# First feed-forward product of the second phase from rounded parts and residues: three float32r products in place of one float32 product

## The reference, cut to what matters

```python
def _layer(x, wqkv, qs, ksc, wo, lg, lb, w1, b1, w2, b2):   # x: (8, 1024, 256), run twice
    ...
    x = x + o @ wo                                   # local attention, output projection
    h = shift_token(x)
    mu = h.mean(-1, keepdims=True)
    var = h.var(-1, keepdims=True)
    h = (h - mu) / jnp.sqrt(var + 1e-05) * lg + lb   # layer norm, 256 channels
    h = h @ w1 + b1                                  # 256 -> 2 * 682, the product that is changed
    a, g = jnp.split(h, 2, axis=-1)
    h = a * jax.nn.gelu(g, approximate=False)
    x = x + h @ w2 + b2
    return x
```

## Time and profile before

| what | value |
|---|---|
| median of 3 runs | 5651.63 us (5647.0 to 5652.35) |
| profiled execution, span | 5649.7 us |
| PE busy | 5488.2 us, 97% of the span |
| DVE, ACT, POOL busy | 73%, 61%, 17% |
| second phase | from about 2711 us to the end |
| second phase, 2840 to 5560 us | PE busy 2699.66 of 2720 us, granted clock 1.00 |

### The profile page before, as it was taken

One profiled execution on the slowest core, in us unless ns is written; L12 is line 12 of the kernel. 1 busy time (PEld: TensorE's weight loads), 2 busy tenths in 40 slices (PEclk: granted clock), 3 DMA queues, 4 the chain that ended last, 5 costly groups with the idle time before them and its releaser, 6 DMA issues.

```text
span 5649.7 us, 145780 instructions
## 1 busy us (share of the span) xinstructions
PE 5488.2 (97%) x57776; PEld 2674.3 (47%) x57776; DVE 4147.2 (73%) x10780; ACT 3455.2 (61%) x6979; POOL 934.9 (17%) x1905
## 2 busy tenths in 40 slices
PE   8999999999999999999799999999999999999998
PEld 3444444444444444433355555555555555555553
DVE  5888878787887888788566666666666777777774
ACT  4676666676666766666455655556555565555654
POOL 2222222222222222222000000000000001010100
PEclk9999999999999999999899999999999999999998
DMA  3333333233333333333100000000000000000000
GB/s 70 55 55 69 54 59 60 50 74 55 65 55 59 63 51 71 55 58 78 44 12 16 8 16 12 12 16 8 16 32 17 18 19 16 19 16 19 19 16 19
DMA packets 128519, 215.62 MB, mean 38 GB/s; under 512 B 40032, under 2 KB 40160, under 8 KB 127072
## 3 DMA queue, kind: packets, MB, share of 16 engines
q1 hardware_dynamic: 127840, 206.30, 18.0%
HBM read 45.73 MB, written 25.17 MB: 13 GB/s over the span
## 4 chain that ended last, share of the span: by engine, by line
PE 72%; ACT 11%; issue 10%; DVE 3%; POOL 3%; DMA 0%; POOLq 0%; SPq 0%; ACTq 0%; DVEq 0%
PE ps L571 23%; PE ps L700 14%; PE ps L821 10%; PE ps L1042 6%; PE ps L1005 5%; PE ps L906 3%; ACT pt L1259 3%; PE ps L898 3%; PE ps L923 3%; ACT gates L1457 1%; ACT sm L1376 1%; PE ps L1007 1%; PE ps L873 1%; PE ps L882 1%; POOL both L2101 1%
## 5 line engine op out<-in xcount | busy, mean ns | idle before, releaser
L1259 ACT ACTIVATE pt<-ps 128x1024 f32<-128x1024 f32 (+7 forms) x2048 | 1237.2, 653 | 620.9 <-PE ps L571 462.9
L700 PE MATMUL ps<-pt,va 128*32 128x512 f32 (+3 forms) x3072 | 1227.5, 487 | 19.9 <-POOL pt L2076 19.9
L700 PE MATMUL ps<-pt,ones 128*32 128x512 f32 (+3 forms) x6144 | 1237.0, 489 | 0.0
L700 PE MATMUL ps<-pt,vs 128*32 128x512 f32 (+3 forms) x3072 | 1231.0, 489 | 0.0
L1633 DVE CUSTOM_DVE_ANT_0 junk<-ps,causal 128x128 bf16<-128x128 f32 (+3 forms) x2048 | 977.8, 487 | 307.2 <-PE ps L571 291.2
L571 PE MATMUL ps<-kt,qt 96*32 96x512 bf16 (+3 forms) x12288 | 1017.0, 329 | 34.9 <-DVE mc L1633 15.9
L571 PE MATMUL ps<-qt,kt 98*32 98x512 bf16 (+3 forms) x12288 | 835.7, 328 | 22.0 <-ACT pt L1259 21.0
L1637 DVE TENSOR_REDUCE mc<-ps 128x1 f32<-128x512 f32 x1024 | 706.3, 690 | 159.2 <-PE ps L571 128.5
L2076 POOL TENSOR_SCALAR_AFFINE_SELECT pt<-pt 128x256 f32<-128x256 f32 x1024 | 467.2, 456 | 1941.1 <-ACT pt L1259 1939.5
L821 PE MATMUL ps<-wqkv,xs 128*128 128x512 f32 x1536 | 727.9, 603 | 0.0
L1376 ACT ACTIVATE sm<-sm,mxw 128x256 f32<-128x256 f32 (+1 forms) x1024 | 493.5, 484 | 241.0 <-DVE mxw L1802 239.6
(11 more groups left out here) (149 smaller groups left out, 8537.9 us busy)
## 6 DMA issues: line engine op xcount, KB each, us to landing
qt<-part SPq DMA_DIRECT2D x768, 64.0 KB, 2.4
kt<-part SPq DMA_DIRECT2D x768, 64.0 KB, 2.5
ya<-wy SPq DMA_DIRECT2D x128, 128.0 KB, 2.3
yb<-wy SPq DMA_DIRECT2D x128, 128.0 KB, 2.3
xs<-between_phases SPq DMA_DIRECT2D x32, 512.0 KB, 3.8
xt<-in_x SPq DMA_DIRECT2D x16, 512.0 KB, 6.5
between_phases<-z SPq DMA_DIRECT2D x16, 512.0 KB, 2.8
between_phases<-xo SPq DMA_DIRECT2D x16, 512.0 KB, 2.8
```

Source lines behind the costliest of these rows:

```text
L700: mmi = pe.matmul(ps[32 * q:32 * q + 32, 4 + half, lo - half * 512:hi - half * 512], w, probs(kb)[:, i, lo - first(kb):hi - first(kb)], st ...
L1259: act.activation(probs(kb)[:, i, kb * P - first(kb):1024 - first(kb)], ps[:, 2 * i:2 * i + 2, :].rearrange("p a q -> p (a q)")[:, kb * P:1 ...
```

## The change

The layer-normed activations and the weights `w1` are both split in two: a part rounded to the type float32r (`cnh`, `w1h`) and the residue to the float32 value, also float32r (`cnl`, `w1l`). One float32 product becomes three products in float32r: part by part, residue of the weights by part, and part by residue of the activations. One tile of two `kc` thus takes six products, 66 for a half. The six are cut in two pieces of three (`W1_PRODUCTS`), which stand where the two `kc` stood, so all other steps of PE keep their places.

New work: ACT runs `scale_bias` four times in place of two (rounded, then float32 in place, for each `kc`); POOL subtracts for each half (`residue`, two of 128x512, in place over `cn`), ahead of the gate window's `combine`, and for each layer splits the weights (`split_w1`, two copies and two subtractions of 128x1408). New waits: the first gate tile waits for both rounded parts (`cnh_done`, signalled after the first and the third of ACT's four steps) and for the weights' residue (`w1l_done`); its second piece waits for both residues (`cnl_done`). The new tiles lie over old ones (`w1l` over `w1`, `cnl` over `cn`, `cnh` over `sqf`); so ACT's step also waits for `ssum_done`.

```diff
+W1_PRODUCTS = (((0, 0, 0, 0), (0, 1, 0, 1), (1, 0, 0, 2)), ((1, 1, 0, 3), (0, 0, 1, 4), (0, 1, 1, 5)))
...
+        w1h = sb("w1h", [P, 2, 2 * HB - 1, P], F32R)
+        w1l = over("w1l", "w1", [P, 2, 2 * HB - 1, P], F32R)
+        cnh = over("cnh", "sqf", [P, 2, 512], F32R)
+        cnl = over("cnl", "cn", [P, 2, 512], F32R)
...
+            def normed(m, n, to, tile, width, parts):
+
+                for part_of in parts:
+                    if n == 0 and part_of == 1:
+                        pe.wait_ge(cnl_done, done(2 * m + 2))
+                    for w, kc, x, k in W1_PRODUCTS[part_of]:
+                        mmi = pe.matmul(to, (w1h, w1l)[w][:, kc, tile, 0:width], (cnh, cnl)[x][:, kc, :],
+                                        start=k == 0, stop=k == 5)
+                return mmi
...
                 elif j == 0:
-                    pe.wait_ge(w1_ready, sent(m // (2 * nb) + 1))
-                    pe.wait_ge(hn_done, done(2 * m + 2))
+                    pe.wait_ge(w1l_done, done(2 * (m // (2 * nb)) + 2))
+                    pe.wait_ge(cnh_done, done(2 * m + 2))
...
-                for kc in kcs:
-                    mmi = pe.matmul(ps[:, fbank(m, 13 + j), :], w1[:, kc, HB - 1 + j, :], cn[:, kc, :], start=kc == 0, stop=kc == 1)
+                mmi = normed(m, HB + j, ps[:, fbank(m, 13 + j), :], HB - 1 + j, P, kcs)
...
+                act.wait_ge(ssum_done, done(m + 1))
                 for kc in range(2):
+                    act.activation(cnh[:, kc, :], cn[:, kc, :], ACT.Identity,
+                                   scale=lnp[:, 0, kc:kc + 1], bias=lnp[:, 1, kc:kc + 1]).then_inc(cnh_done, 1)
                     act.activation(cn[:, kc, :], cn[:, kc, :], ACT.Identity,
                                    scale=lnp[:, 0, kc:kc + 1], bias=lnp[:, 1, kc:kc + 1]).then_inc(hn_done, 1)
...
+            def split_w1(l):
+                pool.wait_ge(w1_ready, sent(l + 1))
+                for kc in range(2):
+                    pool.tensor_copy(w1h[:, kc, :, :], w1[:, kc, :, :]).then_inc(w1h_done, 1)
+                for kc in range(2):
+                    pool.wait_ge(w1h_done, done(2 * l + kc + 1))
+                    pool.tensor_tensor(w1l[:, kc, :, :], w1[:, kc, :, :], w1h[:, kc, :, :], ALU.subtract).then_inc(w1l_done, 1)
+
+            def residue(m):
+                for kc in range(2):
+                    pool.wait_ge(cnh_done, done(2 * m + kc + 1))
+                    pool.wait_ge(hn_done, done(2 * m + kc + 1))
+                    pool.tensor_tensor(cnl[:, kc, :], cn[:, kc, :], cnh[:, kc, :], ALU.subtract).then_inc(cnl_done, 1)
...
+                if m >= 0 and W % 4 == 1:
+                    residue(m)
                 if W + 1 < LAST:
                     combine(W + 1)
...
+                if W == 3:
+                    split_w1(0)
+                if W == 4 * FIRST + 3:
+                    split_w1(1)
```

More of the change, by code:

```diff
@@ L8 @@
 BF16 = mybir.dt.bfloat16
+F32R = mybir.dt.float32r
 ALU = mybir.AluOpType
@@ L145, in program @@
         top = [nc.sbuf_base]
+        place = {}
         def sb(name, shape, dt):
@@ L153, in sb, with over @@
             top[0] = at + n
+            place[name] = at
             return nc.alloc_sbuf_tensor_at(name, shape, dt, offset=at)
+        def over(name, other, shape, dt):
+            return nc.alloc_sbuf_tensor_at(name, shape, dt, offset=place[other])
         def sem(name):
@@ L361, in program @@
         hn_done = sem("hn_done")
+        cnh_done = sem("cnh_done")
+        cnl_done = sem("cnl_done")
+        w1h_done = sem("w1h_done")
+        w1l_done = sem("w1l_done")
         g_full = sem("g_full")
@@ L1002, in gate @@
                     pe.wait_ge(gv_done, done(m * HB + j - 1))
-                for kc in kcs:
[L1004 to L1008, removed]
+                if j < HB - 1:
+                    mmi = normed(m, j, ps[:, fbank(m, 6 + j), :], j, P, kcs)
+                else:
+                    mmi = normed(m, j, ps[0:HPAIR, fbank(m, 6 + j), :], 2 * HB - 2, HPAIR, kcs)
                 if kcs[-1] == 1:
```

## The result

The changed kernel takes 5666.48 us (5663.23 to 5669.94, 7 runs) where the kernel before takes 5650.51: a ratio of 1.0028, interval [1.0018, 1.0038]. It is slower by 16 us, 0.28%, and the interval leaves out 1; the forecast was 5648 and no change. In later series the kernel before stood at 5648.6 to 5650.7.

A forecast was written before the change was run, and what follows sets the result against it. PE was taken as full, with ACT right behind it in both windows. Terms: 17 x 0.21 - 14 x 0.6 + 31 x 0.1 - 2 = -3.7 us, giving 5648; forecast's own range 5634 to 5662, with slower residue 5634 to 5695.

The forecast's parts named there:

- Prices: On PE, a float32r product takes 0.22 us against 0.86, weight load hidden; a half's products go from 18.9 to 14.5 us.
- the rule of the Trainium skill that the prediction names: Weight loads on PE overlap running matmuls only where the row group differs, so none here would be hidden: about +280 us.
- a dearer product: Rival, PE's products: 0.43 us each gives 5980 us, an unhidden load (0.41) 5930; chance 0.13.
- a slower residue: Rival, gate window's first tile: POOL's subtraction takes longer than 1.28 us and PE waits, 5665 to 5690 us; chance 0.17.
- not as said: Rival, PE's products: the chip treats float32r as float32, 38 us more a half, 6860 us; chance 0.01.
- Gate windows: Windows with the first two tiles: 0.21 us lost without `final_mean` (17 halves), 0.6 gained with it (14 halves).
- The wait for DVE before the transposes of the queries: In the gate window, new PE idle time of about 0.5 us before these transposes.
- Hidden windows: Four and a half tiles in 31 halves: PE still waits for ACT, idling 2.2 us; 0.1 us lost each.
- PE's work is the time: Rival, whole kernel: the waits fit elsewhere and 141 us come back, giving 5511 us; chance 0.04.
- The last half: The final half, alone: 4.4 us less products, 0.7 + 2.0 waits; 2 us gained, give or take 4.
- The weights' splitting: POOL's four steps of 3.5 us, 14 for a layer: hidden in 22.23 us of POOL idle time if `w1` lands by 2813.
- at most those 14 once: Cost in us of POOL's weight splitting if the transfer of `w1` doesn't land by 2813.

## Why the prediction was wrong

*Prices: right.* 0.23 for the 0.22 taken; by the prediction's own rate (0.18 us a half for each 0.01) that is +5.6 in the sum. The load is hidden, as rows 9 said: 0.23 is less than the 0.41 of a product and a load one after the other. That is against the rule of the Trainium skill that the prediction names. The residue takes 1.28 as taken, so the rivals of a dearer product, a slower residue and "not as said" fall. (PE's busy time is lower by 3% of the stretch where some 5% was forecast; products dearer by 0.01 are about 0.9 of that, and the rest isn't followed up.)

*Gate windows: right, a little small.* +0.40 and -0.46 for +0.21 and -0.6. Fifteen products on the chain at 0.01 more are 0.15 each: 0.36 and -0.45. The wait for DVE before the transposes of the queries, 0.5 in the forecast, is only 0.14 (2862.14 to 2862.28): the dearer products bring PE there later. (The 2.6 of work saved that the prediction names for this window is 2.4, 12 x 0.86 less 36 x 0.22; it enters no sum.)

*Hidden windows: right.* +0.01 for +0.1. The idle time ahead of the copy, 1.15 for 2.2, is shorter because 27 dearer products take 0.3 more and a wait of 0.31 for DVE stands among them, which the forecast didn't have; the copy itself comes when it came. That ACT's chain ends them is shown by the run without table loads and by the copy that stayed at 15.4 with a third of the products. So "PE's work is the time" falls too, though PE is busy 96%.

*The last half:* the trace from the last window's start to the end is 3.2 shorter; 2 was forecast.

*The weights' splitting: wrong, and this is the step that failed.* The prediction called it hidden because POOL had 22 us idle and its next step wasn't late. Both were so. But the step asked only who waits for POOL, and not what POOL's instructions do to another engine while they run: DVE's two additions, 1.23 each, stood 4.18 and 4.05 beside POOL's subtractions, and PE waited for them. Price 14.5: 6.6 in the first window, 7.9 in the second, of which 3.4 is the lower clock behind the wait. The figure "at most those 14 once" is near that by chance; it stood for POOL being late, which didn't happen. It is luck too that 5666 lies in the range: its upper part stood there for a slower residue. The run with one wait more shows it: the same instructions a few microseconds later, and 12 us are back. No rival had this mechanism; those that would make the kernel slower were about the residue and the product.

Together: +0.7 + 14.5 - 3.2, and 3.4 for the two single falls of the clock, are 15.4; the medians differ by 16.0. The profiled spans differ by 12.9, because in that execution of the changed kernel the first phase, which the change doesn't touch, ended 2.85 earlier (12.9 + 2.85 = 15.75).

## To carry to other kernels

When a step is moved into another engine's idle time, look at what the engines beside it do in those microseconds: here long POOL instructions made DVE's instructions with two inputs from the on-chip memory take up to 4.18 for 1.23, and one wait that put them behind gave 12 of the 16 us back. An engine that is busy 96 to 99% can still be a hair from waiting: price cheaper work on it only up to the next engine's chain, and mend that chain with it, or the gain stays there. Taking work from PE beyond that point can cost time: with a third of the products in the hidden window the granted clock was 0.50 behind PE's longer waits, and the kernel 45 us slower.

## What the runs showed of the hardware that I had not expected

- DVE's 1.23 us addition took 4.18 beside POOL's 128x1408 subtraction, and POOL's subtraction 3.15 alone but up to 4.14 beside DVE: by these times each waits for the other, in turn, instruction by instruction. In a train of 128-column subtractions DVE didn't get its turn at all, in either layer. DVE's 128x512 instructions with one of two inputs in PSUM kept their 0.68 in the changed kernel, beside POOL or not.
- With a third of the products in the hidden window, the granted clock was 0.50 behind PE's first wait of about 2 us there and through the second, and the windows grew by 1.74 (without `final_mean`) and 2.06 (with it) at the median; in the changed kernel, with waits of 1.15 there, one hidden window of 31 showed a fall. So less work for PE made the kernel some 45 us slower than the changed one.
